# Scaling the routed heads' exponentials on GpSimd instead of VectorE, in a fused two-layer attention kernel

## The chip, the cores and the metric

The kernel runs on one core of one Trainium2 chip. The metric is the device time of one execution in microseconds (us); lower is better. The five engines of the core are called TensorE (PE in the profile; its weight loads are PEld), VectorE (DVE), ScalarE (ACT), GpSimd (POOL) and SyncE (SP). They run side by side, each through its own instructions in the order written, and meet only at semaphores.

## What is computed

Eight batches of a 512 x 256 input pass through two gated blocks: attention over a context of 1601 rows (A), routed self-attention (B), a second attention over the context with 16 heads of width 16 (C), and a routed feed-forward network (D). The change is in B:

```
dist = softmax(mean(x @ Wr + br, axis=1))
idx = sort(top_k(dist, 4))                       # 4 of 16 heads of width 64, one choice for each batch
score = softmax((Qs @ Ks^T) / sqrt(64))          # 512 x 512 for each of the 4 heads
O = score @ Vs
x = x + tanh(g_ffn[0]) * (O @ Wo + bo)
```

A head's 512 x 512 scores are handled in four blocks of 128 rows, so B has 16 score blocks of 128 x 512 in each batch and 128 in the whole kernel.

## The kernel before

C of batch b is the backbone. It is laid out as 208 steps (u = 0 to 207, four groups of 52). In a step TensorE makes one transposed score tile of C (`scores_t`, L1687), ScalarE its exponential (`attend`, L1184), and every fourth step TensorE weighs values (`values_c`, L1704). Between them lie "pieces": score chunks of the next group (`scores_c`, L1656), of which VectorE takes row maxima (`maxima`, L2265). A, B and the projections of the next batches are hung into the same steps by tables written out by hand. Every engine walks the same steps and looks in the tables for what is due, so the order of each engine's work is fixed.

B of batch n = b + 1 is prepared during C of batch b. Its tables are `U_SB` (79, 84, 89, 94, 102, 107, 112, 117: the step in which pair k of score blocks is made) and `U_TB` (six and eight steps later: the transposes of the two blocks). For block i of pair k = i // 2, with s = SB[k]:

- s: TensorE `score_b` (L1424) makes both blocks in PSUM; it waits until the exponentials of the pair before are done, since a pair reuses the same two banks
- s+1, s+2: VectorE `max_b` (L2082) takes the negated row maximum
- s+2, s+3: ScalarE `exp_b` (L1063) writes the exponentials into `pB[i % 4]` in SBUF and their row sums into a column of `rsB`
- s+4, s+5: VectorE `normalise`: a reciprocal of the 128 sums (L2087), then a tensor_scalar of 128 x 512 that multiplies `pB` in place by it (L2089)
- s+6, s+8: TensorE `turn_b` (L1439) transposes the block, four 128 x 128 parts
- s+7, s+9: ScalarE `evac_pb` (L1071) copies the transpose to SBUF; later TensorE multiplies it with the values (`weigh_b`, L1447)

`turn_b` stands in TensorE's queue ahead of the next step's `scores_t`; in ScalarE's queue the exponential of a step comes first, then `evac_pb`, then `exp_b`.

Batch 0's B is prepared in an opening phase with tables of its own (`FIRST`). The other seven batches use `LOOP` or `LAST`, which have the same B steps.

GpSimd has root powers for the layer norms (`root`, L872), splits of the keys (`split_k`, L878 and L880), two additions for each batch (L895, L903), and many DMA issues. Between step 71 (`root` of the norm of A) and step 129 (mask loads) its queue is empty in batches whose B is prepared in the loop.

Of the kernel before, what the change touches and what calls it, by code (L numbers as in the profile page):

```python
# [13 lines left out]
ALU = mybir.AluOpType  # L14
# [257 lines left out]
def turn_b_bank(n, i):  # L272

    return (F2, SB[0])[i % 2] if n == 0 else F2
# [7 lines left out]
def norm_a(n):  # L282

    return (0, 2)[n] if n < 2 else 4 * n - 3


def norm_b(n):

    return 4 * n if n else 1


def norm_c(n):

    return (4 * n + 2 if n < B - 1 else 4 * n + 1) if n else 3
# [12 lines left out]
def flamingo(nc, a):  # L307
    ctx_stack = ExitStack()
    with ctx_stack:
        def sem(name):  # L310
            return ctx_stack.enter_context(nc.semaphore(name))

        def sb(name, shape, dt):
            return ctx_stack.enter_context(nc.sbuf_tensor(name, shape, dt))
# [38 lines left out]
        rsB = sb("rsB", [P, ACTIVE * QT], F32)  # L353
# [49 lines left out]
        pB = [take([S], F32) for _ in range(4)]  # L403
# [125 lines left out]
        for i in range(1, 5):  # L529
# [42 lines left out]
        pe_qB, v_qB, pe_kB, a_kB, pe_vB, a_vB, pe_sB, v_nmB, a_expB, v_pB, pe_tB, a_ptB, pe_pvB, v_otB, pe_oB, v_oB = (  # L572
            sem(n) for n in ("pe_qB", "v_qB", "pe_kB", "a_kB", "pe_vB", "a_vB", "pe_sB", "v_nmB", "a_expB", "v_pB",
                             "pe_tB", "a_ptB", "pe_pvB", "v_otB", "pe_oB", "v_oB"))
# [8 lines left out]
        v_self, g_self = sem("v_self"), sem("g_self")  # L583
# [8 lines left out]
        pe_xsT, v_xsT, pe_h, a_h, pe_y, v_y = (sem(n) for n in ("pe_xsT", "v_xsT", "pe_h", "a_h", "pe_y", "v_y"))  # L592
        ys_stored = [sem(f"ys_stored{i}") for i in range(2)]
        v_wt, v_raw, pe_head, v_rk = sem("v_wt"), sem("v_raw"), sem("pe_head"), sem("v_rk")

        NK, NW = 3, 14

# [239 lines left out]
        def _(pool):  # L837
# [32 lines left out]
            def root(L):  # L870
                pool.wait_ge(v_var, L + 1)
                pool.tensor_tensor(rstd[:], vpe[:], mhalf[:], ALU.pow).then_inc(g_rstd, 1)  # L872

            def split_k(n, u):
                w = M_CH[u % NCH][1]
                pool.wait_ge(v_kr, 8 * n + u + 1)
                pool.nop(nofuse=True)
                pool.tensor_copy(k_parts(n, u)[:, 1, 0:w], kr[u % 2][:, 0:w]).then_inc(g_self, 1)  # L878
                pool.wait_ge(g_self, 8 * n + u + 1)
                pool.tensor_tensor(k_parts(n, u)[:, 2, 0:w], kr[u % 2][:, 0:w], k_parts(n, u)[:, 1, 0:w],  # L880
                                   ALU.subtract).then_inc(g_ks, 1)
# [15 lines left out]
            def prepare(n, u, p):  # L897

                if u == p.LB + 3:
                    root(norm_b(n))  # L900
                if u == p.XB[0] + 1:
                    pool.wait_ge(v_xn, 4 * norm_b(n) + 4)
                    pool.tensor_tensor(xw, xw, boB[:].unsqueeze(1).broadcast_to([P, QT, D]), ALU.add).then_inc(g_xb, 1)  # L903
                if u == p.LC + 3:
                    root(norm_c(n))
                for i in range(2 * NCH):
                    if u == p.K[i] + 3:
                        split_k(n, i)
# [56 lines left out]
            for w in range(W_END):  # L965
                prepare(0, w, FIRST)
                start_next(0, w, FIRST)
                start_next(1, w, SECOND)
                if w == 118:
                    pool.wait_ge(v_mT, 2)  # L970
                    pool.partition_all_reduce(small[:, 32:33], small[:, 20:21], P,
                                              bass.bass_isa.ReduceOp.max).then_inc(g_set, 1)
# [22 lines left out]
            for b in range(B):  # L995
                for u in range(NU):
                    if b >= 1:
                        give_out(b, u)
                    if b == B - 1 and u == U_RAMP:
                        ramps()  # L1000
                    if u == U_LD + 9:
                        keep_residual(b)
                    if b + 1 < B:
                        prepare(b + 1, u, plan(b + 1))
                    if b + 2 < B:
                        start_next(b + 2, u, LOOP)
                    if b == B - 1 and u == U_IDS + 4:
                        for j in range(XB):
                            fetch(j)
# [237 lines left out]
        def _(pe):  # L1247
# [177 lines left out]
                       start=True, stop=True).then_inc(pe_sB, 1)  # L1425

            def turn_b(n, i):
                pe.wait_ge(v_pB, 16 * n + i + 1)
                if n == 0 and i < 2:
                    pe.wait_ge(a_vB, 2)  # L1430
                    pe.wait_ge(a_xT, 2 * norm_a(1) + 2)
                elif n == 0:
                    pe.wait_ge(a_ptB, i - 1)
                elif i == 8:
                    pe.wait_ge(v_otB, 2 * n + 1)
                elif i:
                    pe.wait_ge(a_ptB, 16 * n + i)
                for k in range(QT):
                    last = tr(PS[:, turn_b_bank(n, i), k * P:(k + 1) * P], pB[i % 4][:, k * P:(k + 1) * P], ident[:])  # L1439
                last.then_inc(pe_tB, 1)  # L1440
# [110 lines left out]
            def prepare(n, u, p, piece=nothing):  # L1551
# [50 lines left out]
                for i in range(16):  # L1602
                    if u == p.TB[i]:
                        turn_b(n, i)
                        piece()
# [344 lines left out]
        def _(dve):  # L1950
            own = Ticks(v_self)
            v = nc.vector
# [131 lines left out]

            def normalise(n, i):
                dve.wait_ge(a_expB, 16 * n + i + 1)
                v.reciprocal(rsB[:, i:i + 1], rsB[:, i:i + 1]).then_inc(*own.tick())  # L2087
                dve.wait_ge(v_self, own.now())
                v.tensor_scalar(pB[i % 4], pB[i % 4], rsB[:, i:i + 1], None, ALU.mult).then_inc(v_pB, 1)  # L2089

            def residual_b(n, j):
                if j == 0:
# [71 lines left out]
            def prepare(n, u, p, piece):  # L2164
# [58 lines left out]
                for i in range(16):  # L2223
                    if u == p.SB[i // 2] + 1 + i % 2:
                        max_b(n, i)
                        piece()
                    if u == p.SB[i // 2] + 4 + i % 2:
                        normalise(n, i)
                        piece()
# [442 lines left out]
```

## Time and profile before

| | us |
|---|---|
| median of 3 runs (lowest, highest) | 2760.3 (2756.8, 2762.64) |
| profiled execution, own time | 2768.3 |
| its span in the profile | 2766.5 |
| VectorE busy | 1719.3 |
| GpSimd busy | 279.8 |

All durations below are from the one profiled execution. Its own time is 1.8 us over its span and 8.0 us over the median of the runs, so differences and not absolute times are carried over to the median.

### The profile page before, as it was taken

What the parts mean: (1) busy time and instruction counts of PE and PEld (TensorE: products, weight loads), DVE (VectorE), ACT (ScalarE), POOL (GpSimd) and SP (SyncE); (2) the same over time, 40 slices, a digit from 0 to 9 for tenths busy, and PEclk for the clock granted to TensorE, in tenths of its full rate; (3) what the DMA queues carried; (4) which work ended last, traced back from release to release, by engine and by line L of the source; (5) the groups of instructions that cost most, each with busy time, mean ns of one, the idle gap of its engine ahead of it and who ended that gap; (6) DMA issues with size and microseconds to landing.
All of it is one profiled execution on the core that took longest, in us unless ns stands there. A gap on an engine that the chain in (4) does not pass through costs nothing.

```text
span 2766.5 us, 39397 instructions
## 1 busy us (share of the span) xinstructions
PE 2626.0 (95%) x13626; PEld 1278.4 (46%) x13626; DVE 1719.3 (62%) x4190; ACT 1448.6 (52%) x2939; POOL 279.8 (10%) x341
## 2 busy tenths in 40 slices
PE   8989999999999999999999999999999999999998
PEld 4543434353345433443445333443345333349997
DVE  3557776567666776567666765677656777853111
ACT  2423565457554656457545655465545755763232
POOL 1200200020001000020002000110002000012221
PEclk9999999999999999999999999999999989999999
DMA  5612413251332313241324123231323122169994
GB/s 211 168 59 47 121 42 92 58 134 22 88 87 67 87 42 113 61 120 40 97 55 115 45 70 105 59 96 43 113 54 90 19 69 59 34 236 374 371 365 162
DMA packets 215525, 296.37 MB, mean 107 GB/s; under 512 B 50533, under 2 KB 181325, under 8 KB 215318
## 3 DMA queue, kind: packets, MB, share of 16 engines
q1 hardware_dynamic: 198428, 222.87, 28.9%
q0 software_dynamic: 16080, 70.16, 7.4%
q8 instruction: 111, 1.82, 0.3%
q10 hardware_dynamic: 816, 0.79, 0.1%
q14 instruction: 90, 0.74, 0.1%
HBM read 232.87 MB, written 60.50 MB: 106 GB/s over the span
## 4 chain that ended last, share of the span: by engine, by line
PE 78%; DVE 9%; ACT 5%; issue 4%; SPq 2%; DMA 1%; POOL 0%; ACTq 0%; POOLq 0%; DVEq 0%
PE PS L1704 12%; PE PS L1656 10%; PE PS L1687 10%; DVE mxC L2265 7%; PE PS L1329 7%; PE PS L1297 7%; PE PS L1839 5%; PE PS L1849 5%; PE PS L1527 2%; PE PS L1424 2%; PE PS L1358 2%; PE PS L1447 2%; PE PS L1315 2%; PE PS L1439 2%; ACT reg L1063 2%
## 5 line engine op out<-in xcount | busy, mean ns | idle before, releaser
L1184 ACT ACTIVATE reg<-PS 128x512 f32<-128x512 f32 (+1 forms) x1664 | 963.2, 599 | 917.8 <-PE PS L1687 912.3
L2265 DVE TENSOR_REDUCE mxC<-PS 128x1 f32<-128x400 f32 (+1 forms) x2048 | 1089.1, 569 | 497.1 <-PE PS L1656 480.6
L1656 PE MATMUL PS<-reg 96*128 96x400 bf16 (+1 forms) x2048 | 664.4, 338 | 25.7 <-DVE mxC L2265 19.0
L1687 PE MATMUL PS<-reg 99*128 99x512 bf16 (+1 forms) x1664 | 610.2, 386 | 20.8 <-ACT reg L1184 19.0
L1704 PE MATMUL PS<-reg 128*17 128x512 f32 (+1 forms) x3328 | 443.7, 605 | 0.8 <-DVE reg L2289 0.4
L1656 PEld LDWEIGHTS PS<-reg 96*128 96x128 bf16 x2048 | 195.0, 98 | 501.2 <-DVE mxC L2265 373.3
L1687 PEld LDWEIGHTS PS<-reg 99*128 99x128 bf16 (+1 forms) x1664 | 164.4, 101 | 354.1 <-ACT reg L1184 197.5
L1297 PE MATMUL PS<-reg 128*128 128x512 f32 (+1 forms) x512 | 205.8, 517 | 14.3 <-DVE small L2014 13.4
L1329 PE MATMUL PS<-reg 128*128 128x512 f32 (+1 forms) x416 | 211.3, 601 | 0.8 <-ACT reg L1047 0.8
L1223 ACT ACTIVATE reg<-PS,reg 128x128 f32<-128x128 f32 x312 | 89.2, 369 | 197.6 <-PE PS L1839 197.6
L1839 PEld LDWEIGHTS PS<-reg 128*128 128x128 f32 x1248 | 145.0, 192 | 2.7 <-issue 0.8
L1839 PE MATMUL PS<-reg 128*128 128x128 f32 x1248 | 146.0, 275 | 0.0
L1849 PE MATMUL PS<-reg 128*128 128x256 f32 x624 | 141.6, 378 | 0.0
L1297 PEld LDWEIGHTS PS<-reg 128*128 128x128 f32 x512 | 88.1, 191 | 82.0 <-issue 52.2
L1704 PEld LDWEIGHTS PS<-reg 128*17 128x17 f32 (+1 forms) x3328 | 55.3, 95 | 145.5 <-issue 107.5
L1849 PEld LDWEIGHTS PS<-reg 128*128 128x128 f32 x624 | 115.2, 189 | 15.0
L872 POOL TENSOR_TENSOR rstd<-vpe,mhalf 128x4 f32<-128x4 f32 x32 | 33.1, 1034 | 879.6 <-DVE vpe L1993 879.5
L2014 DVE CUSTOM_DVE_ANT_0 reg<-PS,reg 128x512 f32<-128x512 f32 (+1 forms) x128 | 72.4, 570 | 75.5 <-PE PS L1297 75.5
L2082 DVE TENSOR_REDUCE nmB<-PS 128x1 f32<-128x512 f32 x128 | 84.8, 682 | 28.2 <-PE PS L1424 28.2
L1358 PE MATMUL PS<-reg,wkC 128*128 128x400 f32 (+1 forms) x256 | 100.5, 502 | 1.6 <-DVE reg L2076 1.6
L1527 PE MATMUL PS<-wvC,reg 128*128 128x256 f32 (+1 forms) x416 | 99.6, 379 | 0.0
L1329 PEld LDWEIGHTS PS<-reg 128*128 128x128 f32 (+1 forms) x416 | 75.9, 192 | 48.4 <-issue 38.3
(269 smaller groups left out, 2493.0 us busy)
## 6 DMA issues: line engine op xcount, KB each, us to landing
reg<-in_D_W SPq DMA_DIRECT2D x78, 1024.0 KB, 8.4
reg<-in_A_mask POOLq DMA_DIRECT2D x30, 800.5 KB, 6.8
dramK<-reg SPq DMA_DIRECT2D x144, 100.0 KB
dramV<-reg SPq DMA_DIRECT2D x48, 272.0 KB, 3.1
reg<-in_ctxT POOLq DMA_DIRECT2D x8, 1601.0 KB, 9.8
reg<-in_ctx POOLq DMA_DIRECT2D x8, 1536.0 KB, 7.8
reg<-dramQ SPq DMA_DIRECT2D x32, 384.0 KB, 5.6
dramQ<-reg SPq DMA_DIRECT2D x90, 128.0 KB
```

The costliest lines, as they stand in the source:

```text
L1184: act.activation(pr[u % RING][0:r, :], PS[0:r, S_PLAN[NU * b + u][0], :], ACT.Exp).then_inc(a_expC, 1)
L1223: act.activation(hT[:, m, :], PS[:, bank, at:at + TS], ACT.Relu, bias=b1[par][:, m:m + 1]).then_inc(a_h, 1)
L1297: last = mm(PS[:, ring_a(n, i), 0:w], qg(n)[:, k, t * P:(t + 1) * P], ctxT[:, k, c0:c0 + w], start=k == 0, stop=k == KD - 1)
L1329: last = mm(PS[:, FB[m], :], ctxN[0:r, c, m * P:(m + 1) * P], ptA[0:r, c, :], start=c == 0, stop=c == CT - 1)
L1358: last = mm(PS[:, k_bank(n, u), 0:w], wkC[:, k, m * P:(m + 1) * P], ctxT[:, k, c0:c0 + w], start=k == 0, stop=k == KD - 1)
L1527: last = mm(PS[0:rows(c), v_bank(n, i), c % 2 * D:(c % 2 + 1) * D], ctxT[:, k, c * P:c * P + rows(c)], wvC[:, k, :], start=k == 0, stop=k ...
L1656: last = mm(PS[:, bank, 0:w], qs[(NG * bb + g) % 3][0:ROWS, h, t * P:(t + 1) * P], ks[g % 2][0:ROWS, h, c0:c0 + w], start=True, stop=True)
L1687: last = mm(PS[0:r, bank, :], ks[g % 2][0:STK, h, c * P:c * P + r], qs[(NG * b + g) % 3][0:STK, h, :], start=True, stop=not with_mask)
L1704: last = mm(PS[32 * h:32 * h + DC + 1, VB, :], vc[0:r, c, g * GH + h, :], pr[(UN * g + GH * c + h) % RING][0:r, :], start=c == 0, stop=c = ...
L1839: last = mm(PS[:, bank, at:at + TS], w1[j % WB][:, k, m * P:(m + 1) * P], xsT[j % 2][:, k, :], start=k == 0, stop=k == KD - 1)
L1849: last = mm(PS[:, VB, 0:D], hT[:, m, :], w2[j % WB][:, m, :], start=m == 0, stop=m == FM - 1)
L2265: v.tensor_reduce(mxC[:, h, t, j:j + 1], PS[:, M_PLAN[bb, g, i][0], 0:M_CH[j][1]], AX.X, ALU.max).then_inc(v_mx, 1)
```

## The change

From the second batch on, VectorE makes only the reciprocal, and GpSimd does the multiplication at the same step of the tables. `turn_b` waits for GpSimd. Batch 0 stays as it was. Two semaphores are added, one from VectorE to GpSimd (`v_rB`), one from GpSimd to TensorE (`g_pB`).

```
+        v_rB, g_pB = sem("v_rB"), sem("g_pB")
...
             def prepare(n, u, p):          # GpSimd
...
+                for i in range(16):
+                    if n and u == p.SB[i // 2] + 4 + i % 2:
+                        pool.wait_ge(v_rB, 16 * (n - 1) + i + 1)
+                        pool.tensor_scalar(pB[i % 4], pB[i % 4], rsB[:, i:i + 1], None, ALU.mult).then_inc(g_pB, 1)
...
             def turn_b(n, i):              # TensorE
-                pe.wait_ge(v_pB, 16 * n + i + 1)
+                if n == 0:
+                    pe.wait_ge(v_pB, i + 1)
+                else:
+                    pe.wait_ge(g_pB, 16 * (n - 1) + i + 1)
...
             def normalise(n, i):           # VectorE
                 dve.wait_ge(a_expB, 16 * n + i + 1)
-                v.reciprocal(rsB[:, i:i + 1], rsB[:, i:i + 1]).then_inc(*own.tick())
-                dve.wait_ge(v_self, own.now())
-                v.tensor_scalar(pB[i % 4], pB[i % 4], rsB[:, i:i + 1], None, ALU.mult).then_inc(v_pB, 1)
+                if n == 0:
+                    v.reciprocal(rsB[:, i:i + 1], rsB[:, i:i + 1]).then_inc(*own.tick())
+                    dve.wait_ge(v_self, own.now())
+                    v.tensor_scalar(pB[i % 4], pB[i % 4], rsB[:, i:i + 1], None, ALU.mult).then_inc(v_pB, 1)
+                else:
+                    v.reciprocal(rsB[:, i:i + 1], rsB[:, i:i + 1]).then_inc(v_rB, 1)
```

## Rows read from the trace of the kernel before

**Rows 1.** The page: each engine's busy time, share of the span, instructions.

```profile
PE 2626.0 (95%) x13626; PEld 1278.4 (46%) x13626; DVE 1719.3 (62%) x4190; ACT 1448.6 (52%) x2939; POOL 279.8 (10%) x341
```

**Rows 2.** The page: the chain that ended last, by engine.

```profile
PE 78%; DVE 9%; ACT 5%; issue 4%; SPq 2%; DMA 1%; POOL 0%; ACTq 0%; POOLq 0%; DVEq 0%
```

**Rows 3.** Busy time by stretch: B's blocks of batch 3; then up to batch 4's.

```profile
944.00:997.00 53.00, 49.24 (x282) 18.23 (x282) 38.34 (x92) 43.07 (x96) 0.00 (x0) 1.00 0.07 13
997.00:1245.70 248.70, 239.39 (x1168) 107.24 (x1166) 165.54 (x406) 127.13 (x234) 25.08 (x30) 1.00 0.34 91
```

**Rows 4.** Groups by line in 944 to 997 us, VectorE then ScalarE.

```profile
L2265 DVE TENSOR_REDUCE mxC<-PS 128x1 f32<-128x400 f32 (+1 forms) x34 | 18.8, 570 | 7.3 <-PE PS L1656 6.5
L2089 DVE TENSOR_SCALAR reg<-reg,rsB 128x512 f32<-128x512 f32 x16 | 7.8, 486 | 0.6
...
L1184 ACT ACTIVATE reg<-PS 128x512 f32<-128x512 f32 (+1 forms) x46 | 27.4, 604 | 9.7 <-PE PS L1687 9.3
```

**Rows 5.** Waits of TensorE's matmuls in 944 to 997 us: total, times, longest.

```profile
PE PS L1439 <- ACT reg L1071: 2.1, 3, 1.0
PE PS L1687 <- ACT reg L1184: 0.8, 2, 0.6
PE PS L1656 <- DVE mxC L2265: 0.3, 1, 0.3
```

**Rows 6.** Timeline, block 2 of batch 3: start, duration, instruction.

```profile
949.81 2.32 DVE L2265 TENSOR_REDUCE mxC<-PS 128x1 f32<-128x401 f32 x4
...
951.74 1.13 PE L1424 MATMUL PS<-reg 64*128 64x512 f32 x4
...
952.04 0.15 DVE L2087 RECIPROCAL rsB<-rsB 128x1 f32<-128x1 f32 x1
952.23 0.49 DVE L2089 TENSOR_SCALAR reg<-reg,rsB 128x512 f32<-128x512 f32 x1
...
952.80 0.39 PE L1687 MATMUL PS<-reg 99*128 99x512 bf16 x1
952.81 0.58 PEld L1439 LDWEIGHTS PS<-ident,reg 128*128 128x128 f32 x4
...
953.03 0.60 PE L1439 MATMUL PS<-ident,reg 128*128 128x128 f32 x4
...
953.47 0.38 PE L1687 MATMUL PS<-reg 99*128 99x512 bf16 x1
...
954.38 0.59 ACT L1071 ACTIVATE reg<-PS 128x512 f32<-128x512 f32 x1
```

**Rows 7.** The chain that ended last, same place.

```profile
952.87 0.32 PE PS L1687
953.19 0.44 PE PS L1439 x4
953.63 0.23 PE PS L1687
...
954.38 0.59 ACT reg L1071
```

**Rows 8.** Timeline, block 12 of batch 3; then block 2 of batch 7.

```profile
987.04 0.49 DVE L2089 TENSOR_SCALAR reg<-reg,rsB 128x512 f32<-128x512 f32 x1
...
987.62 0.58 PEld L1439 LDWEIGHTS PS<-ident,reg 128*128 128x128 f32 x4
...
2158.85 0.49 DVE L2089 TENSOR_SCALAR reg<-reg,rsB 128x512 f32<-128x512 f32 x1
...
2159.43 0.58 PEld L1439 LDWEIGHTS PS<-ident,reg 128*128 128x128 f32 x4
```

**Rows 9.** Timeline, block 0 of batch 3.

```profile
945.91 0.15 DVE L2087 RECIPROCAL rsB<-rsB 128x1 f32<-128x1 f32 x1
...
947.75 0.53 PEld L1439 LDWEIGHTS PS<-ident,reg 128*128 128x128 f32 x4
947.92 0.60 PE L1439 MATMUL PS<-ident,reg 128*128 128x128 f32 x4
```

**Rows 10.** GpSimd's groups over the whole span.

```profile
L880 POOL TENSOR_TENSOR reg<-reg 128x400 bf16<-128x400 f32 x48 | 43.9, 914 | 3.9
...
L878 POOL CAST reg<-reg 128x400 bf16<-128x400 f32 x48 | 24.8, 516 | 148.9 <-DVE reg L2076 148.8
```

**Rows 11.** Timeline: a VectorE instruction and the GpSimd one waiting for it.

```profile
1182.59 0.63 DVE L2076 SCALAR_TENSOR_TENSOR reg<-PS,bkC,reg 128x400 f32<-128x400 f32 x1
...
1183.35 0.52 POOL L878 CAST reg<-reg 128x400 bf16<-128x400 f32 x1 [4.23 <-DVE reg L2076]
```

## The prediction

> **What bounds the kernel.** I read the page's busy times and its chain first. TensorE is busy 95% of the span and VectorE 62% [rows 1]; the chain that ended last is 78% TensorE, 9% VectorE, 5% ScalarE and 0% GpSimd [rows 2]. So a VectorE instruction is worth its duration only where TensorE stands still for it, and the place to look is the stretch in which B's sixteen blocks are made. The windows give it: about 53 us in a batch, seven times. In batch 3's stretch TensorE is busy 49.2 us, ScalarE 43.1, VectorE 38.3 and GpSimd 0; outside it, in 248.7 us, the change touches nothing [rows 3]. The reader is to see three things there. VectorE has 14.7 us of air in 53. GpSimd is empty. TensorE's matmuls wait 0.3 us for VectorE's maxima and 2.9 us for ScalarE (2.1 + 0.8) [rows 5]. ScalarE in turn stands idle 9.3 us for TensorE's transposed scores, and VectorE 6.5 us for TensorE's score chunks [rows 4]. TensorE and ScalarE hand work to each other; VectorE follows.
>
> **What is removed.** 16 tensor_scalars of 0.486 us in a batch [rows 4], 7 batches: 112 x 0.486 = 54.4 us of VectorE's time. I take this as worth nothing. The cover is VectorE's own air: it waits for TensorE before and after, and what follows the scaling, the row maxima of the next pair, is not what releases ScalarE. At block 2 the second scaling would end 0.5 us sooner, but the exponential that needs the maximum stands in ScalarE's queue behind a copy that starts at 954.38 [rows 6]. Were the cover gone, the most that TensorE could get back is what it waits for VectorE's maxima, 0.3 us in a batch [rows 5]: 7 x 0.3 = 2.1 us. The reciprocals stay, and with them VectorE's wait for the row sums.
>
> **What is added.** The multiplication is now a GpSimd instruction between two hand-overs, and the question is for which of the 16 transposes it comes too late. Before, with R the start of the reciprocal of block 2 (952.04), the scaling ends at R+0.68 and the transpose's first weight load starts at R+0.77, 0.09 us after it [rows 6]. That is an immediate release: this transpose really waits for the scaling. Block 12 shows the same 0.09 us (987.04 + 0.49 = 987.53, then 987.62), and so does block 2 of batch 7 [rows 8]; I count these two blocks in each of the seven batches, 14 in all. The next tightest kind is block 0, where the load starts at R+1.84 (945.91 to 947.75) [rows 9]; the other 13 blocks have at least about that much. The reason why block 2 is tight is in the same rows: VectorE is behind with four maxima from 949.81 on [rows 6], so its reciprocal comes late. The change doesn't move that: none of the removed scalings lies in that run of maxima.
>
> After, the load can start at R + 0.15 (reciprocal) + h1 + T + h2. h1, VectorE to GpSimd, is 0.13 us: L2076 ends at 1183.22, the waiting cast starts at 1183.35 [rows 11]. h2, to TensorE, is taken as the 0.09 us of today's release [rows 6]; no row shows GpSimd releasing TensorE. So the load starts at R + 0.37 + T.
>
> T, a GpSimd tensor_scalar of 128 x 512 in fp32, isn't in the trace. The nearest rows are a cast of 128 x 400 with one tensor input, 0.516 us, and a tensor_tensor of 128 x 400 with two, 0.914 us [rows 10]. By columns (x 1.28) they give 0.66 and 1.17. I take 0.66, since the new instruction has one tensor input like the cast, and keep 1.17 as the far end; from below, VectorE's own 0.49 bounds it. The load then starts at R+1.03. The first matmul followed its load by 0.17 us where nothing was queued ahead (947.75, 947.92) [rows 9], so at R+1.20, where before it started at R+0.99 (953.03), behind the score matmul of 952.80 [rows 6]. The delay is 0.21 us. With T = 1.17 it is 0.72, with T = 0.49 it is 0.04.
>
> Does TensorE's delay pass on? Behind `turn_b` in its queue stands the next transposed score, L1687 at 953.47 [rows 6], and ScalarE waits for it; then come the copy at 954.38 and the next pair's exponential, which releases the next `score_b`. The chain that ended last runs through just these: L1687, L1439, L1687, then ScalarE's L1071 [rows 7]. So I count the delay in full: 14 x 0.21 = 2.9 us, say 3. At the far end 14 x 0.72 = 10.1 us, at the near one 14 x 0.04 = 0.6 us. A block like block 0 is reached only when 0.37 + T passes 1.84, T = 1.47, beyond the far end. Two scalings in a row don't collide either: with T = 0.66 the second of the pair is done about 1.4 us after the first began, and its transpose comes two steps later.
>
> GpSimd's queue: behind the new waits stand only the mask loads of step 129 and the root of step 138. The mask loads wait for `weigh_b` of the same blocks anyway, so nothing becomes later through the queue itself. No DMA is moved.
>
> **Two rules of the skill.** In the stretch VectorE's work is reductions out of PSUM, 34 of them the maxima, beside the sixteen scalings that leave it [rows 4]; that GpSimd and VectorE get in each other's way there is nothing that these rows show. The Trainium skill (SBUF — State Buffer, Who interferes with whom) says that the two share a port pair as an exclusive lock, and that a reduction never takes it on this chip: by that rule the new instructions run free, and the sum stays. The rows of GpSimd's cast and tensor_tensor differ by a factor of 1.8 at one size [rows 10]. The Trainium skill (GPSIMD Engine Reference, 4.1 Engine selection) calls two-input elementwise work about twice as slow on GpSimd and one-input work roughly line-rate; its general rule against elementwise work there would give the second rival.
>
> **The rivals.**
>
> 1. Faster: VectorE's relief pulls the exponentials forward. Its place is the pair's cycle `score_b`, `max_b`, `exp_b`, `score_b`. For it speaks that VectorE runs late by four maxima at block 2 [rows 6] and holds 9% of the chain [rows 2]. Against it: 0.3 us of wait in the stretch [rows 5]. If one cycle a batch were bound by VectorE, it would shorten by two scalings, 0.97 us: 7 x 0.97 = 6.8, less the 2.9, about 4 us faster, 2756. It decides as soon as more than 0.4 us a batch (2.9 / 7) comes back; two cycles a batch would give 2750.
> 2. Clearly slower: GpSimd is slow at it, T of about 0.97 (twice 0.486) to 1.17. Each delay is 0.97 + 0.37 + 0.17 - 0.99 = 0.52 us or 0.72: 14 of them are 7.3 to 10.1 us, 2767.6 to 2770.4. For it: the two-input row, and that the operation works in place on fp32, twice the output bytes of the cast. Against: only one tensor is read.
> 3. No change: the delay is absorbed, since ScalarE stands idle 9.3 us a batch [rows 4] and TensorE waits for it later anyway. Then 2760.3, within 1 us. Against it the chain passes through the very transpose [rows 7].
>
> **How the numbers follow.** The profiled execution was 2768.3 us and would become 2771.3; taken to the median, 2760.3 + 3.0 = 2763.3. 0.2% is 5.5 us, about what a measurement of this kernel can tell from no change. My forecast (T between 0.5 and 0.84, plus 0.6 to 5.5 us; its own range 2761 to 2766) has 0.47; rival 3 has 0.10; rival 2 with all T above 0.84 has 0.31; rival 1 has 0.12, of which 0.10 is beyond 0.2% if two cycles or more are bound. So faster 0.10, within 0.2% 0.59, slower 0.31. The range reaches to rival 1's first figure and to the far end of T with a little for the spread of runs: 2756 to 2771.
>
> **What would show it.** Right: GpSimd has a new group of 112 at about 0.66 us and is busy about 74 us more; L2089 is down to 16; TensorE's load of L1439 at blocks 2 and 12 starts about 0.26 us later after the reciprocal and waits for GpSimd; a batch takes about 0.4 us more. Wrong: T over 0.84; a third block in a batch waiting for GpSimd; or batches that get shorter, with ScalarE's exponentials of the next pair earlier than before.

## The result, and the profile after

The changed kernel takes 2772.33 us (median of 6 runs, 2767.64 to 2775.96) against 2760.52 us before (6 runs, 2756.8 to 2764.24): the ratio is 1.004, with a 95% interval of 1.003 to 1.005. It is slower by 0.4%, 11.8 us, where I had forecast 3 us. It lies above my range (to 2771), on the side to which I had given a chance of 0.31.

The profiled spans differ by 4.3 us only (2766.5 and 2770.8). The mean granted clock of TensorE is 0.992 in the profiled run of before and 0.995 in that of after, and the shortfalls lie ahead of and behind the seven repeated stretches: 0.98 in the first 340 us of both, 0.97 before and 0.99 after behind 2160 and 2165 us, and 1.00 between. So I read what lies between, where both profiles are at the full clock.

The page after, busy times and chain by engine, which answer to [rows 1, 2]:

```profile
PE 2621.0 (95%) x13626; PEld 1277.1 (46%) x13626; DVE 1667.9 (60%) x4078; ACT 1446.6 (52%) x2939; POOL 454.2 (16%) x453
...
PE 79%; DVE 10%; ACT 4%; issue 4%; POOL 1%; SPq 1%; DMA 1%; ACTq 0%; POOLq 0%; DVEq 0%
```

VectorE lost 51 us of work and GpSimd took on 174, three times as much. GpSimd now stands in the chain that ended last. Its groups by line, of the whole span, say why:

```profile
L908 POOL TENSOR_SCALAR reg<-reg,rsB 128x512 f32<-128x512 f32 x112 | 174.2, 1563 | 325.3 <-DVE rsB L2100 325.3
L881 POOL TENSOR_TENSOR reg<-reg 128x400 bf16<-128x400 f32 x48 | 43.8, 913 | 3.8
...
L879 POOL CAST reg<-reg 128x400 bf16<-128x400 f32 x48 | 24.7, 514 | 148.8 <-DVE reg L2084 148.8
```

One scaling takes 1.563 us. I had taken 0.66, with 1.17 as the far end; the old rows of the cast and the tensor_tensor are unchanged.

Busy time by stretch, B's blocks of batch 3 and then up to batch 4's (as in [rows 3]: length, then busy us and instructions of PE, PEld, DVE, ACT and POOL, granted clock, DMA share, GB/s):

```profile
945.22:1000.08 54.86, 49.67 (x282) 18.26 (x282) 30.92 (x76) 43.02 (x96) 24.88 (x16) 1.00 0.06 12
1000.08:1249.06 248.98, 239.40 (x1168) 107.28 (x1166) 165.77 (x406) 127.06 (x235) 25.11 (x30) 1.00 0.34 91
```

The stretch grew from 53.0 to 54.9 us, with TensorE's and ScalarE's work as before and VectorE at 30.9 us instead of 38.3. The rest of the batch, 248.7 and 249.0 us, takes about what it took. The timeline of block 2, to be laid beside [rows 6]:

```profile
952.95 1.13 PE L1429 MATMUL PS<-reg 64*128 64x512 f32 x4
...
953.26 0.21 DVE L2100 RECIPROCAL rsB<-rsB 128x1 f32<-128x1 f32 x2
953.51 3.10 POOL L908 TENSOR_SCALAR reg<-reg,rsB 128x512 f32<-128x512 f32 x2 [3.01 <-DVE rsB L2100]
...
954.02 0.39 PE L1695 MATMUL PS<-reg 99*128 99x512 bf16 x1
954.11 0.69 DVE L2090 TENSOR_REDUCE nmB<-PS 128x1 f32<-128x512 f32 x1 [0.64 <-PE PS L1429]
955.13 0.42 PEld L1447 LDWEIGHTS PS<-ident,reg 128*128 128x128 f32 x4 [1.02 <-POOL reg L908]
955.13 0.66 PE L1447 MATMUL PS<-ident,reg 128*128 128x128 f32 x4 [0.72 <-POOL reg L908]
...
955.62 0.38 PE L1695 MATMUL PS<-reg 99*128 99x512 bf16 x1
...
956.53 0.59 ACT L1076 ACTIVATE reg<-PS 128x512 f32<-128x512 f32 x1
```

With R = 953.26, the start of the reciprocal, the scaling starts at R+0.25 and ends at R+1.82, and load and first matmul of the transpose start together at R+1.87, where they started at R+0.77 and R+0.99. The matmul is 0.88 us late. The copy on ScalarE starts 3.27 us after R and not 2.34, so 0.93 us late: the delay passes on in full. VectorE takes the next maximum early and waits 0.64 us for TensorE first: its relief became idle time.

How often this happens is in the waits of the whole span (total, times, longest):

```profile
PEld PS L1447 <- POOL reg L908: 30.6, 35, 1.3
...
PE PS L1447 <- POOL reg L908: 10.1, 14, 0.7
```

TensorE's matmuls wait for GpSimd 14 times, two in each of seven batches, as counted in the prediction. Weight loads are put down to GpSimd 35 times, 35 / 7 = five in a batch, but not all five wait for it. They are those of blocks 0, 2, 4, 9 and 12. At blocks 4 and 9 GpSimd had ended 0.55 and 0.71 us before the load, which starts where it started in the kernel before (R+2.36 and R+2.52). At block 0 the load is released by GpSimd, 0.04 us later than before. Block 14, not among the five, has its load 0.05 us later too. The matmuls of these two blocks do not move (in the last batch block 0's moves by 0.09 us). And the chain at that place, where [rows 7] had none of GpSimd:

```profile
953.51 1.57 POOL reg L908
...
955.13 0.66 PE PS L1447 x4
955.78 0.23 PE PS L1695
...
956.53 0.59 ACT reg L1076
```

For the experiments I use one more measure, the time from batch to batch: the distance of the first matmuls of block 0's transpose in neighbouring batches, from batch 1 to batch 7. These are the first and the last in the timeline before, then after:

```profile
345.06 0.60 PE L1439 MATMUL PS<-ident,reg 128*128 128x128 f32 x4
...
2154.53 0.60 PE L1439 MATMUL PS<-ident,reg 128*128 128x128 f32 x4
```

```profile
342.51 0.60 PE L1447 MATMUL PS<-ident,reg 128*128 128x128 f32 x4
...
2163.12 0.65 PE L1447 MATMUL PS<-ident,reg 128*128 128x128 f32 x4
```

(2154.53 - 345.06) / 6 = 301.6 us before and (2163.12 - 342.51) / 6 = 303.4 us after. Single distances can be 0.3 to 1.5 us longer, in e7_exp_together one by 3 us, also in kernels in which GpSimd scales nothing, so below I give the median of the six, 301.44 and 303.32: 1.88 us a batch, 13.2 us in seven, against 11.8 measured (8 to 14 by the interval).

### The profile page after: what moved, and what is told of

It is laid out like the page before. It is cut to its first block, busy times and chain, and to the rows that moved or that the text cites. A ratio compares the mean times of both kernels' runs of the same rounds, so it can differ in the third digit from the quotient of the medians.

```text
span 2770.8 us, 39397 instructions
## 1 busy us (share of the span) xinstructions
PE 2621.0 (95%) x13626; PEld 1277.1 (46%) x13626; DVE 1667.9 (60%) x4078; ACT 1446.6 (52%) x2939; POOL 454.2 (16%) x453
## 3 DMA queue, kind: packets, MB, share of 16 engines
q8 instruction: 111, 1.82, 0.3%
## 4 chain that ended last, share of the span: by engine, by line
PE 79%; DVE 10%; ACT 4%; issue 4%; POOL 1%; SPq 1%; DMA 1%; ACTq 0%; POOLq 0%; DVEq 0%
PE PS L1712 12%; PE PS L1664 11%; PE PS L1695 10%; DVE mxC L2276 7%; PE PS L1334 7%; PE PS L1302 7%; PE PS L1847 5%; PE PS L1857 5%; PE PS L1535 3%; PE PS L1363 3%; PE PS L1455 2%; PE PS L1447 2%; PE PS L1429 2%; PE PS L1320 2%; ACT reg L1189 1%
## 5 line engine op out<-in xcount | busy, mean ns | idle before, releaser
L908 POOL TENSOR_SCALAR reg<-reg,rsB 128x512 f32<-128x512 f32 x112 | 174.2, 1563 | 325.3 <-DVE rsB L2100 325.3
L1447 PE MATMUL PS<-ident,reg 128*128 128x128 f32 x512 | 78.7, 278 | 27.3 <-ACT reg L1076 16.2
```

The lines of the kernel that those rows point to most:

```text
L908: pool.tensor_scalar(pB[i % 4], pB[i % 4], rsB[:, i:i + 1], None, ALU.mult).then_inc(g_pB, 1)
```

## The experiments

The figures of all runs in one place. T is the mean duration of GpSimd's instruction on `pB`; "batch" is the median time from batch to batch in the profiled execution; the ratio is to the kernel before, with its interval. Four kernels were run only once, so that they have a profile but no ratio.

| run | T, us | batch, us | ratio (95%) |
|---|---|---|---|
| before | - | 301.44 | 1 |
| changed kernel | 1.563 | 303.32 | 1.004 (1.003 to 1.005) |
| e1_keep_2_12 | 1.563 | 301.43 | 0.9997 (0.9986 to 1.0009) |
| e2_only_2_12 | 1.836 | 303.91 | 1.0075 (1.0059 to 1.009) |
| e3_constant | 1.489 | 303.15 | run once |
| e4_broadcast | 1.041 | 302.23 | 1.0015 (1.0003 to 1.0027) |
| e5_no_scaling | - | 301.44 | 0.9998 (0.9988 to 1.0009) |
| e6_later_turn | 1.56 | 302.99 | 1.0034 (1.0022 to 1.0046) |
| e7_exp_together | - | 303.36 | 1.0054 (1.0039 to 1.007) |
| e8_copies_on_vector | 1.56 | 301.94 | 1.0015 (1.0003 to 1.0026) |
| e9_half_columns | 0.923 | 302.01 | run once |
| e10_copy | 0.613 | 301.50 | run once |
| e11_halves | 1.034 | 302.47 | run once |
| e12_early_reciprocal | 1.562 | 301.45 | 0.9998 (0.9988 to 1.0008) |

### Which blocks cost

**e1_keep_2_12.** Edit, in short:

```
+ON_G = (0, 1, 3, 4, ..., 11, 13, 14, 15)
-                    if n and u == p.SB[i // 2] + 4 + i % 2:
+                    if n and i in ON_G and u == p.SB[i // 2] + 4 + i % 2:
```

with the waits counted to match, and VectorE scaling the other two blocks.

> Blocks 2 and 12 of each batch stay on VectorE, the other 14 are scaled on GpSimd. In the changed kernel the GpSimd scaling took 1.56 us and the time from batch to batch went from 301.6 to 303.4 us. Theory A (all of the loss is the late start of the transposes of blocks 2 and 12, twice 0.93 us in a batch): the batch is back at 301.6 us and the ratio to the kernel before is 1.000. Theory B (GpSimd's work costs something at every block, by its port or by its queue, about 1.8 us spread over 16 blocks): 14 of 16 parts stay, about 1.6 us in a batch, ratio 1.004. Block 14 may then wait some hundredths of a us for GpSimd, which either theory allows.

Measured: 301.43 us and 0.9997. Fourteen of sixteen scalings on GpSimd, 98 x 1.563 = 153 us of its time, cost nothing.

**e2_only_2_12.** The same edit with `ON_G = (2, 12)`.

> The other way round: only blocks 2 and 12 go to GpSimd, 14 blocks stay on VectorE. Theory A: 2 x 0.93 x 7 = 13 us more than before, ratio 1.004 to 1.005, as in the changed kernel, although VectorE is relieved of 14 scalings only. Theory B: 2 of 16 parts, 0.2 us in a batch, ratio 1.001.

Measured: 303.91 us and 1.0075. The ratio is above the 1.004 to 1.005 that I expected. Two scalings a batch carry all of the loss, and more of it: 2.5 us a batch and not 1.9. The additional part is in T. GpSimd's group here, and the timeline of block 2 of batch 3:

```profile
L910 POOL TENSOR_SCALAR reg<-reg,rsB 128x512 f32<-128x512 f32 x14 | 25.7, 1836 | 425.4 <-DVE rsB L2104 425.4
```

```profile
958.05 0.49 DVE L2102 TENSOR_SCALAR reg<-reg,rsB 128x512 f32<-128x512 f32 x1
958.06 1.83 POOL L910 TENSOR_SCALAR reg<-reg,rsB 128x512 f32<-128x512 f32 x1 [25.47 <-DVE rsB L2104]
```

VectorE's scaling of block 3 starts at the same moment as GpSimd's of block 2. VectorE's takes its usual 0.49 us, GpSimd's 1.83 instead of 1.56, and so it is at all 14 (1.833 to 1.844). That GpSimd stood idle for 25 us and more before each is not the cause: in the changed kernel the first scaling of batch 3 comes after 19 us of idle time too and takes 1.57 us. The overlap cannot happen there, since VectorE has no such scaling. So the two engines do get in each other's way where both scale at once; e11_halves shows the same in another form. The timed difference, 20.7 us by the ratio (16 to 25), holds the 7 x 2.47 = 17.3 us of the batches.

### What VectorE's relief is worth

**e5_no_scaling.** Nobody scales from the second batch on; the division by the sums is left out.

```
-                        pool.wait_ge(v_rB, 16 * (n - 1) + i + 1)
-                        pool.tensor_scalar(pB[i % 4], pB[i % 4], rsB[:, i:i + 1], None, ALU.mult).then_inc(g_pB, 1)
...
-                    pe.wait_ge(g_pB, 16 * (n - 1) + i + 1)
+                    pe.wait_ge(v_rB, 16 * (n - 1) + i + 1)
```

> From the second batch on nobody scales: the product with the reciprocal sums is left out, the reciprocals stay, and the transposes wait for them. It tells what the 54 us of VectorE's time that the change removes are worth by themselves. My theory, that VectorE is covered in this stretch: 0 to 2 us faster than before, ratio 0.999 to 1.000. The rival, that VectorE's relief pulls the next pair forward: 7 us or more faster, ratio 0.997 or less.

Measured: 301.44 us, to the hundredth that of before, and 0.9998. The 54 us of VectorE's scalings are worth nothing here; the rival that the relief pulls the pairs forward is dead.

### Whether the start or the duration sets the delay

**e12_early_reciprocal.** The reciprocals of even blocks stand one step earlier in VectorE's table:

```
-                    if u == p.SB[i // 2] + 4 + i % 2:
+                    if u == p.SB[i // 2] + (3 if n and i % 2 == 0 else 4) + i % 2:
                         normalise(n, i)
```

> The changed kernel with one edit on VectorE: from the second batch on the reciprocals of the even blocks are due one step earlier, in the midst of VectorE's run of row maxima. The theory says that blocks 2 and 12 are late because their reciprocal starts 1.5 us after their sums are there (VectorE is behind with four maxima), and GpSimd's 1.56 us then come on top. With the reciprocal 1 us or more earlier, GpSimd ends before TensorE asks, and the batch goes from 303.4 us back to 301.5, ratio to the kernel before 1.000. If it stays at 303.4, it is not the start of the scaling that sets the transposes. One more way: VectorE now stands still for the sums ahead of its maxima, and the batch comes out between the two.

Measured: 301.45 us and 0.9998, with GpSimd's scaling as slow as ever (1.562 us). The timeline of block 2 of batch 3:

```profile
948.27 0.16 DVE L2100 RECIPROCAL rsB<-rsB 128x1 f32<-128x1 f32 x1 [0.19 <-ACT reg L1068]
...
948.36 1.57 DVE L2276 TENSOR_REDUCE mxC<-PS 128x1 f32<-128x400 f32 x3
...
948.53 3.12 POOL L908 TENSOR_SCALAR reg<-reg,rsB 128x512 f32<-128x512 f32 x2 [2.02 <-DVE rsB L2100]
...
950.53 0.58 PEld L1447 LDWEIGHTS PS<-ident,reg 128*128 128x128 f32 x4
...
950.75 0.49 PE L1447 MATMUL PS<-ident,reg 128*128 128x128 f32 x3
```

The reciprocal now stands ahead of three of the maxima and waits 0.19 us for its sums. GpSimd is done with block 2 at about 948.53 + 1.56 = 950.09, before TensorE asks at 950.53. The reciprocals of the other even blocks moved too, but only blocks 2 and 12 had a delay to lose. So both parts are needed for the loss: VectorE's run of maxima, which makes the reciprocal late, and GpSimd's 1.56 us.

**e6_later_turn.** The transposes of blocks 2, 3, 12 and 13 ask one step later:

```
+U_TB = [t + (i in (2, 3, 12, 13)) for i, t in enumerate(U_TB)]
```

> The changed kernel with the transposes of blocks 2, 3, 12 and 13 one step later in the table. If the loss is only that the transposes of blocks 2 and 12 ask too early, a step of about 1 us covers the 0.88 us and the batch returns to 301.6 us, ratio to the kernel before 1.000 (0.999 to 1.001). If a late transpose costs because the next pair cannot start (its banks, its exponentials), the delay comes back elsewhere in the pair's cycle and the ratio stays at 1.003 to 1.004.

Measured: 302.99 us and 1.0034, so the hopeful reading fell and the other one held. The timeline of block 2 of batch 3:

```profile
954.06 0.69 ACT L1069 ACTIVATE reg<-PS,nmB 128x512 f32<-128x512 f32 x1
...
955.58 0.60 ACT L1190 ACTIVATE reg<-PS 128x512 f32<-128x512 f32 x1 [0.74 <-PE PS L1696]
...
956.07 0.59 ACT L1077 ACTIVATE reg<-PS 128x512 f32<-128x512 f32 x1
956.55 0.69 ACT L1069 ACTIVATE reg<-PS,nmB 128x512 f32<-128x512 f32 x1
...
956.81 0.63 PE L1448 MATMUL PS<-ident,reg 128*128 128x128 f32 x4 [0.70 <-ACT reg L1077]
```

The copy of block 2 (L1077) now stands between the two exponentials of the next pair (L1069), where it stood ahead of both. The second exponential, which releases the next pair's scores, is behind it. Counted from block 0's transpose, the first exponential starts 0.66 us earlier than in the kernel before, the second 0.66 us later, and the next pair's scores 0.87 us later. A transpose that is asked for later is a late copy, and a late copy is a late exponential, by waiting or by the table.

### Why GpSimd takes 1.56 us

**e3_constant.** A constant in place of the value for each partition (the division by the sums is left out):

```
-                        pool.tensor_scalar(pB[i % 4], pB[i % 4], rsB[:, i:i + 1], None, ALU.mult).then_inc(g_pB, 1)
+                        pool.tensor_scalar(pB[i % 4], pB[i % 4], 0.002, None, ALU.mult).then_inc(g_pB, 1)
```

> GpSimd multiplies by the constant 0.002 and not by the reciprocals, so the division by the sums is left out from the second batch on; everything else is as in the changed kernel. The 128 x 512 tensor_tensor with a broadcast took 1.04 us, the tensor_scalar with a value for each partition 1.56. Theory P (the value for each partition is what makes it slow): about 0.66 us, the figure that my prediction took from the cast by columns, and blocks 2 and 12 start about as before, 301.6 to 302.0 us from batch to batch. Theory Q (GpSimd's tensor_scalar itself is slow at this size, whatever the operand): 1.56 us and 303.4 us.

**e4_broadcast.** In its place stands `pool.tensor_tensor(pB[i % 4], pB[i % 4], rsB[:, i:i + 1].broadcast_to([P, S]), ALU.mult)`.

> GpSimd multiplies with a tensor_tensor whose second input is the reciprocal broadcast over 512 columns. If the price is that of the operation's form, the rows of GpSimd's other tensor_tensors (0.914 us for 400 columns, 2.00 for 1024) give 1.1 to 1.17 us, and with hand-overs of 0.09 and 0.05 us the transposes of blocks 2 and 12 start 1.45 us after the reciprocal's start, 0.46 later than before: 14 x 0.46 = 6.4 us more than before, ratio 1.002. If the price is that of 512 fp32 columns read and written in place on GpSimd, it stays at 1.56 us and the ratio at 1.004.

**e9_half_columns.** The tensor_scalar has `pB[i % 4][:, 0:S // 2]` as input and output.

> GpSimd scales 256 of the 512 columns, the others stay unscaled. Constant price for each column: half of 1.56, 0.8 us. A large fixed part: between 1.0 and 1.5 us. At 0.8 us blocks 2 and 12 start (0.8 + 0.15 + 0.09 + 0.05) = 1.1 us after the reciprocal's start, 0.1 later than before, and a batch takes 301.7 us.

**e10_copy.** In place of the tensor_scalar stands `pool.tensor_copy(pB[i % 4], pB[i % 4])`.

> GpSimd copies each block onto itself instead of scaling it, so the division by the sums is left out. My prediction took 0.66 us for the scaling from a cast of 400 columns by the number of columns. If that step was sound for an operation with one input, the copy takes 0.6 to 0.7 us, and only tensor_scalar is the exception; if reading and writing 512 fp32 columns in place is what costs, it takes 1.0 us or more.

GpSimd's group of each, in this order:

```profile
L908 POOL TENSOR_SCALAR reg<-reg 128x512 f32<-128x512 f32 x112 | 165.5, 1489 | 331.5 <-DVE rsB L2100 331.5
```

```profile
L908 POOL TENSOR_TENSOR reg<-reg,rsB 128x512 f32<-128x512 f32 x112 | 115.1, 1041 | 369.2 <-DVE rsB L2100 368.4
```

```profile
L908 POOL TENSOR_SCALAR reg<-reg,rsB 128x256 f32<-128x256 f32 x112 | 102.7, 923 | 378.7 <-DVE rsB L2100 378.5
```

```profile
L908 POOL COPY reg<-reg 128x512 f32<-128x512 f32 x112 | 67.1, 613 | 405.6 <-DVE rsB L2100 405.6
```

Against what was expected: the constant takes nearly as long (Theory Q, with 1.49 for 1.56 us); the broadcast goes by the price of the form, a little under my 1.1 to 1.17 us; the half lies between my two cases, so part of its time is fixed, but less than I had allowed for. The copy takes 0.613 us, near the 0.66 that my step from the cast gave: reading and writing 512 fp32 columns in place is not what costs. The value for each partition costs 0.07 us (1.563 against 1.489). What is left is the operation. If the time is a fixed part and a price for each column, tensor_scalar takes (1.563 - 0.923) / 256 = 2.5 ns a column and 0.28 us fixed; this is an estimate from two sizes. The same product written as a tensor_tensor is a third shorter, with two inputs. Why this engine's tensor_scalar is slow no run here shows.

These runs are also four more sizes of the same delay. The prediction counts the lateness of blocks 2 and 12 in full, twice in a batch, and that can be read off. ScalarE's copy of block 2's transpose starts 0.00 us (e10_copy), 0.29 (e9_half_columns), 0.39 (e4_broadcast), 0.85 (e3_constant), 0.93 (changed kernel) and 1.21 us (e2_only_2_12) later after R than in the kernel before. Twice that is 0.00, 0.58, 0.78, 1.70, 1.86 and 2.42 us; the batches are longer by 0.06, 0.57, 0.79, 1.71, 1.88 and 2.47. By the duration: T = 0.613 gives 0.06 us a batch, 0.923 gives 0.57, 1.041 gives 0.79, 1.489 gives 1.71, 1.563 gives 1.88. From 0.923 on it is a line: 1.88 - 0.57 = 1.31 us a batch for 0.64 us of T, two for one. The timed ratio of e4_broadcast, 1.0015, is 4.1 us with an interval from 0.8 to 7.5, which holds 7 x 0.79 = 5.5 us.

### Two engines on one block, and what else the freed time could do

**e11_halves.** VectorE scales columns 0 to 255 and GpSimd the others, both after the reciprocal.

> Each block is shared out: VectorE scales the first 256 columns, GpSimd the other 256 at the same time. Where only GpSimd's other scalings overlap one of VectorE's (only blocks 2 and 12 on GpSimd) the instruction took 1.84 us and not 1.56. If the two get in each other's way, GpSimd's half takes longer than the same half alone by up to VectorE's own duration (0.3 us), or VectorE's does; if not, both take what they take alone. A batch would then take 301.6 to 302.2 us.

```profile
L908 POOL TENSOR_SCALAR reg<-reg,rsB 128x256 f32<-128x256 f32 x112 | 115.3, 1034 | 369.8 <-DVE rsB L2101 369.3
```

Measured: GpSimd's half takes 1.034 us in the mean, 0.11 more than the same size alone, VectorE's 0.359; the batch 302.47 us, above my 301.6 to 302.2. The mean is of two kinds. In 77 of the 112, those of blocks 2 and 12 among them, GpSimd starts while VectorE's half is still running, and takes 1.08 us. Most of the others start behind it and take 0.92 as alone. With 1.08 us, and a start of the load 0.07 us behind its end, the copy of block 2 is 0.47 us late, and twice that is most of the 1.03 us a batch. Sharing doesn't pay.

**e8_copies_on_vector.** e1_keep_2_12, with ScalarE's copies of the eight even transposes (`evac_pb`) moved to VectorE as a tensor_copy.

> Blocks 2 and 12 are scaled on VectorE and the other 14 on GpSimd, and the time so freed on VectorE takes over ScalarE's copies of the eight even transposes (0.59 us each there; a tensor_scalar out of PSUM of this size took 0.74 us on VectorE). If ScalarE's queue sets the pace of the stretch, 8 x 0.49 = 3.9 us a batch leave it, of which I expect a quarter to a half to come back: 7 to 14 us faster, ratio 0.995 to 0.998. If TensorE's order and the hand-overs set it, 1.000; if VectorE is now late with the row maxima, above 1.

Measured: 301.94 us and 1.0015. Taking work from ScalarE bought nothing. The waits of TensorE's matmuls in the whole span:

```profile
PE PS L1687 <- DVE npt L2311: 15.7, 12, 3.5
...
PE PS L1453 <- DVE reg L2116: 10.0, 21, 0.7
```

In e1_keep_2_12 it waits for `npt`, which VectorE makes from the row maxima, 5 times and 9.7 us; here it waits once more in each of the seven batches, 0.84 us each time. The waits of `turn_b` for ScalarE's copies (16.2 us there) are now mostly waits for VectorE's (L1453, 10.0). So VectorE is late, as in the third case above; that this makes the 0.5 us a batch was not tested apart.

**e7_exp_together.** The kernel before, with one edit on ScalarE:

```
-                    if u == p.SB[i // 2] + 2 + i % 2:
+                    if u == p.SB[i // 2] + 2 + (i % 2 if n == 0 else 0):
                         exp_b(n, i)
```

> The kernel before, VectorE scaling everything, with one edit on ScalarE: from the second batch on the exponentials of both blocks of a pair come in the same step, the second one ahead of the next step's transposed scores instead of behind them. I hold that the pair's cycle runs over ScalarE's exponentials and TensorE's waits for them (0.5 to 0.6 us before a pair's scores), and not over VectorE. Then the next pair's scores start earlier, up to 0.3 us a pair: 7 batches x 6 pairs x 0.2 = 8 us faster, ratio 0.997. The rival: ScalarE is merely full, and what the pair gains the backbone's exponential loses, ratio 1.000 or somewhat above.

Measured: 303.36 us and 1.0054, the wrong way; the rival came true. The timeline in batch 3:

```profile
956.42 0.39 PE L1687 MATMUL PS<-reg 99*128 99x512 bf16 x1 [0.31 <-ACT reg L1184]
```

This matmul of a transposed score stands ahead of the next pair's scores and waits 0.31 us for the backbone's exponential, now behind the second one of the pair. Counted from block 0's transpose, that second exponential ends 0.49 us earlier than in the kernel before, and the next pair's scores start 0.32 us later. So the exponentials did not release them. The 0.5 to 0.6 us that I had gone by are idle times of the weight load ahead of them; no matmul of `score_b` waits for ScalarE in the waits of the kernel before. My reading, not tested apart, is that the backbone loses more than the pair gains. No experiment here gave a kernel that is faster than before by more than the interval.

## Why the prediction was wrong

The step that failed is one term: T, the duration of GpSimd's tensor_scalar of 128 x 512. I took 0.66 us "since the new instruction has one tensor input like the cast", and kept 1.17 us "as the far end". It takes 1.563. e10_copy shows that the scaling by columns was sound for a copy (0.613), and e3_constant and e4_broadcast that the number of inputs is not what sorts GpSimd's operations: a tensor_scalar with no second input at all takes 1.49 us, a tensor_tensor 1.04. The far end was no bound, because it bounded one operation by another one. Why tensor_scalar takes that long stays open.

The steps around it held, but for one small one.

- What VectorE's relief is worth: nothing, as said; e5_no_scaling has it at 0.00 us a batch.
- Which blocks: 2 and 12, 14 in all; the waits count 14, e1 and e2 confirm it from both sides.
- Why these: VectorE behind with four maxima. e12 takes the reciprocal out from behind three of them and the loss is gone.
- The hand-overs: 0.13 and 0.09 us predicted; 0.10 and 0.05 measured (R+0.15 to R+0.25; R+1.82 to R+1.87).
- The delay passes on in full: 0.88 us at the transpose, 0.93 at the copy, twice in a batch 1.88.

The small one that was off: I let the first matmul follow its load by 0.17 us, "where nothing was queued ahead". I misread the place, for a score chunk was ahead of it:

```profile
947.75 0.34 PE L1656 MATMUL PS<-reg 96*128 96x400 bf16 x1
```

After a long wait the matmul starts with its load (955.13 both). By my sum a T of 0.613 us makes the matmul 0.16 us late; in e10_copy it starts where it started before (R+0.99), still behind the score matmul. So my 3 us would not have come out with T = 0.66 either: by the batches of e10_copy and of e9_half_columns (0.06 us for T = 0.613, 0.57 for 0.923) I estimate about 1 us.

With the measured T the prediction's own formula gives a load at R + 0.37 + 1.56 = R+1.93, a matmul at R+2.10, 1.11 us late, and 14 x 1.11 = 15.5 us; with the two corrections 14 x 0.88 = 12.3. The median moved by 11.8.

I also said that a third kind of block would be reached at T = 1.47. It was: the loads of blocks 0 and 14 wait for GpSimd and start 0.04 and 0.05 us later, but their matmuls do not move, since they stand behind other matmuls. So it cost nothing. I had named a third block that waits as a sign of being wrong; it was there, and it was harmless.

Rival 2 was the right mechanism, with a T that even it did not reach (it ended at 2770.4 us). The Trainium skill (GPSIMD Engine Reference, 4.1 Engine selection) has one-input work on GpSimd at roughly line-rate; the copy roughly fits that (0.613 us, where VectorE scales the same block in 0.487) and the tensor_scalar, at 1.563 us, doesn't, so here the measurement decides. The Trainium skill (SBUF — State Buffer, Who interferes with whom) lets reductions and GpSimd run side by side; the traces agree, T being 1.55 to 1.58 us in the changed kernel whatever the maxima beside it, and where VectorE's own tensor_scalar ran beside it, it rose to 1.83.

## What to carry to other kernels

Before work is moved to an engine, find in the trace the consumer that starts right behind it (here 0.09 us) and those that have slack: 14 of 16 blocks could take a scaling that ends 1.1 us later without a trace of it in the time, and two could take 0.15 us (e10_copy) but not 0.5 (e9_half_columns). A duration for an operation that the trace doesn't have must not be bounded by other operations of the engine; where it decides the sign, say that it is unbounded upwards, or time it first. When a slow step cannot be made shorter, starting it earlier in the queue of the engine ahead (one step, e12) can hide it whole, while letting its consumer ask later (e6) moved the delay on.

## What the runs showed of the hardware

- GpSimd's tensor_scalar in fp32 is the slowest of its operations on this block seen here: 1.563 us for 128 x 512 with a value for each partition, 1.489 with a constant, 0.923 for 256 columns, against 1.041 for a tensor_tensor of 128 x 512 with a broadcast second input and 0.613 for a copy of 128 x 512.
- A GpSimd tensor_scalar that starts together with one of VectorE's (0.49 us) takes 1.83 us and not 1.56, and VectorE's is not lengthened. In halves, GpSimd's 256 columns take 1.08 us where they overlap VectorE's 256 and 0.923 alone.
